# First attention of a two-layer transformer program: row maxima from 40 of 120 contraction rows, two heads in two halves of the array, causal mask added by TensorE

## Chip, core and metric

One core of a Trainium2 chip runs one launch that computes the whole program. The time is the device time of that launch in microseconds (us). Engines are named as in the profile: PE is TensorE's matmul side and PEld its weight loads, DVE is VectorE, ACT is ScalarE, POOL is GpSimd, SP is SyncE, which here only issues DMAs.

## The reference, cut to what matters

Two attention layers and two mixture-of-experts layers follow one another, each added to `x`. The change touches the first attention alone, with B = 4 sequences of T = 1024 rows of 128 values, 16 heads, each with 8 content and 32 rotary dimensions:

```python
q = jnp.concatenate([q_content, q_rope], axis=-1)      # 40 values per head
k = jnp.concatenate([k_content, k_rope], axis=-1)
scores = jnp.einsum('bhqd,bhkd->bhqk', q, k) * scale
scores = jnp.where(causal[None, None], scores, jnp.float32(-jnp.inf))
attn = jax.nn.softmax(scores, axis=-1)
out = jnp.einsum('bhqk,bhkd->bhqd', attn, v)
```

The softmax subtracts a row maximum from each score before the exponential. Any number near the maximum serves there, since it cancels between numerator and denominator.

## The kernel before

**Units.** The first attention works on 32 units: a unit is two heads of one sequence (`NU = 8 * B`). A score is a product of two fp32 numbers, each split into a high and a low part in TensorE's fp32r format. The tiles `Qp` and `Kp` (four buffers each, 128 partitions x 2 heads x 1024 columns) hold these parts stacked along the contraction: partitions 64 to 103 hold the 40 high parts of a head, 0 to 63 and 104 to 119 the cross terms high x low and low x high, and partition 120 the row maximum (against ones on the other side). SP ships them there from the rotary and content tiles with 16 DMAs per unit (L484).

**Items.** An order written out in Python (`Attn0.order`) lists the items of all engines. Per unit there are 12 `mx` items, 12 `st` items, one `mxT`, and 6 `pv`. Nearly all use a ring of three PSUM tiles `S0` to `S2` (128 x 1024, two banks, one per head): an item may be written only when the item three places earlier in the ring has been read. `mx` and `st` alternate in it, so an `mx` waits for ACT's reading of an `st` and an `st` waits for DVE's reading of an `mx`.

- `mx` (L548): queries x keys for both heads, one matmul per head with contraction over 120 partitions, to find row maxima of a unit two ahead of the one attended. Of a unit's 12 `mx` items, 4 are full (512 columns per head, no mask) and 8 are diagonal: their last 128 columns hold the causal triangle, and they have 128, 256, 384 or 512 columns, twice each.
- DVE reads a full item with one reduction over both heads (L760, to `first`). For a diagonal item it runs one fused instruction per head (L765) that adds the mask tile `later` (128 x 512, zeros and then the triangle), takes the maximum and writes the sum back to PSUM; each is followed by a short read of the accumulator into `mx`.
- `mxT` (L553, L776, L828): the maxima are transposed, negated, and sent by a DMA on POOL's queue into partition 120 of `Qp`.
- `st` (L559): keys x queries with contraction over 121 partitions, so the maximum is already taken off; ACT exponentiates it into `P` (L653), POOL zeroes the triangle (L836).
- `pv` (L577): P x V after every second `st`; four matmuls with 9 output columns each, placed in four column strips of the array.
- `ao`, `oT`: the sums are copied, transposed (L583) and divided (L785 to L791). For the next half sequence, `rope` (L540, L741 to L747, L824), `v`, `cq`, `ck` and the layer norm run beside it, and routing of earlier sequences (L233 to L307).

The lowest line that the change moves at the start is L672, a memset of `later` on DVE; `mqk`, the triangle, is loaded by SP at L462.

Of the kernel before, what the change touches and what calls it, by code (L numbers as in the profile page):

```python
# [313 lines left out]
NU = 8 * B  # L314
EARLY = 3
# [13 lines left out]
class Attn0:  # L329
    names = ("wkd", "wvd", "wo0")  # L330

    def __init__(self, p, st, route):
# [11 lines left out]
        self.later = sb("later", [128, 512])  # L344
# [112 lines left out]
def attn0_sync(p, k, sp, ye):  # L457
# [3 lines left out]
    for t, n in ((k.cos[:], "cos"), (k.sin[:], "sin"), (k.R["ck"][:], "wkr"), (k.later[:, 384:512], "mqk")):  # L461
        ye.dma_start(t, a[n]).then_inc(p.sem("d_c").h, 16)  # L462
# [4 lines left out]
    for u in range(NU):  # L467
        b, group = u // 8, u // 4
        if u >= 4:
            sp.wait_ge(p.made("st"), 12 * (u - 3))  # L470
        for name, tiles, high in (("cq", k.Q, 0), ("ck", k.K, 1)):
            dst = tiles[u % 4]
            if group:
                sp.wait_ge(p.sem("g_rope_l"), 4 * group - (2 if name == "cq" else 0))
            else:
                sp.wait_ge(p.sem("v_rope_l"), 2 if name == "cq" else 4)
            sp.wait_ge(p.done(name), b + 1)
            for h in range(2):
                r, q = 16 * (2 * u % 8 + h), 8 * (2 * u % 16 + h)
                rope, content = k.RH[name][r:r + 16].bitcast(F32), k.CH[name][q:q + 8].bitcast(F32)  # L480
                for at, many, src in ((64, 2, rope[:, high]), (96, 1, content[:, high:high + 1]), (104, 2, content),
                                      (0, 4, rope.rearrange("p a b t -> p (a b) t"))):
                    rows = dst[at:at + many * src.shape[0], h, :].bitcast(F32)
                    ye.dma_start(rows, src).then_inc(p.sem(f"d_q{u % 4}").h, 16)  # L484
# [5 lines left out]
def attn0_tensor(p, k, pe, te):  # L490
    S, A, W = p.S, p.A, k.W
    for w in k.items:
# [49 lines left out]
        elif w.kind == "mx":  # L542
# [4 lines left out]
            for h in range(2):  # L547
                ins = te.matmul(S[s][:, 512 * h:512 * h + n], Q[0:120, h, 128 * qt:128 * qt + 128],  # L548
                                K[0:120, h, 512 * part:512 * part + n], start=True, stop=True)
# [120 lines left out]
def attn0_vector(p, k, dve, ve):  # L670
    S, x = p.S, p.x
    ve.memset(k.later[:, 0:384], 0.0)  # L672
# [5 lines left out]
    for w in k.items:  # L678
# [75 lines left out]
        elif w.kind == "mx":  # L754
# [8 lines left out]
            for h in range(2):  # L763
                of = S[s][:, 512 * h:512 * h + n]
                ins = ve.tensor_tensor_reduce(out=of, in0=of, in1=k.later[:, 512 - n:512], scale=1.0, scalar=-3e38, op0=ALU.add, op1=ALU.max,  # L765
                                              accum_out=k.mx[:, h, qt:qt + 1])
# [1441 lines left out]
```

## Time and profile before

| | us |
|---|---|
| three runs | 1746.73, 1750.57, 1753.07 (median 1750.57) |
| the profiled execution | 1747.28 |
| its span, first to last instruction | 1745.5 |
| first attention in steady state | about 81 to 918 of the span |
| PE busy over the span | 1377.1 (79%) |
| DVE busy over the span | 1127.0 (65%) |
| granted TensorE clock, mean | 0.868 of 2.4 GHz |

Busy time is what the records of an engine cover. A matmul's record includes its way through the array, so a busy PE can still be waiting for nothing but latency. The clock has two levels, 1.2 and 2.4 GHz; a granted clock of 0.95 over a stretch means that it was at the lower one for a tenth of it. The chain follows the work that ended last back from the end; its shares tell which engine's work set the time.

### The profile page before, as it was taken

Reading aid. Unit: us, or ns where it says so; the run is one execution under the profiler, and the core shown is the slowest. Engines: PE = TensorE matmul, PEld = TensorE weight load, DVE = VectorE, ACT = ScalarE, POOL = GpSimd, SP = SyncE. Lnnn points to the kernel's source line nnn. Section 1 sums busy time; section 2 is a strip of 40 time slices with the busy share of each in tenths; the row PEclk is TensorE's granted clock in tenths of the full one; section 3 lists DMA queues with packets and bytes.
Section 4 is the critical chain, followed back from the end, with each engine's and each line's share of the span. In section 5 each row is a group of like instructions: output and inputs, shape, how many; then the busy total and the mean of one; then the engine's idle time right before and its main releaser. Section 6 shows DMA issues by size and latency. Waiting matters only on the chain.

```text
span 1745.5 us, 36985 instructions
## 1 busy us (share of the span) xinstructions
PE 1377.1 (79%) x13404; PEld 896.9 (51%) x13404; DVE 1127.0 (65%) x3630; ACT 703.9 (40%) x1139; POOL 688.7 (39%) x1004
## 2 busy tenths in 40 slices
PE   3487888878888888787886799959899984877881
PEld 2243434444344444443544566637677773665671
DVE  4477686776767767777673554438888775444556
ACT  1044444534444444444453033425544441113673
POOL 3022232232332332323222123357976763564664
PEclk9699999989999989999898699968988885556996
DMA  4645616356164461553702401111221112112334
GB/s 103 94 79 83 100 24 106 57 87 99 24 102 64 73 111 20 86 88 54 125 11 99 142 28 33 40 44 52 56 60 34 33 34 97 33 38 73 89 89 160
DMA packets 74151, 123.23 MB, mean 71 GB/s; under 512 B 17680, under 2 KB 46359, under 8 KB 73076
## 3 DMA queue, kind: packets, MB, share of 16 engines
q1 hardware_dynamic: 65252, 106.81, 32.2%
q0 software_dynamic: 7616, 13.59, 2.3%
q8 instruction: 109, 1.79, 0.4%
q10 hardware_dynamic: 1104, 0.48, 0.1%
q14 instruction: 70, 0.57, 0.1%
HBM read 30.47 MB, written 17.60 MB: 28 GB/s over the span
## 4 chain that ended last, share of the span: by engine, by line
PE 54%; DVE 21%; issue 6%; DMA 6%; SPq 5%; ACT 4%; POOL 3%; DVEq 0%; ACTq 0%; POOLq 0%
PE S L548 5%; DVE first L760 5%; PE A L577 5%; PE S L1016 4%; SPq L484 4%; PE S L540 4%; PE S L559 4%; PE S L1336 3%; DVE S L765 3%; PE A L1347 3%; PE S L168 2%; DMA Kp<-rck 2%; DVE tB L742 2%; PE S L1353 2%; PE A L1028 2%
## 5 line engine op out<-in xcount | busy, mean ns | idle before, releaser
L653 ACT ACTIVATE P<-S 128x1024 f32<-128x1024 f32 (+3 forms) x384 | 309.7, 809 | 406.1 <-PE S L559 403.0
L836 POOL TENSOR_SCALAR_AFFINE_SELECT P<-P 128x256 f32<-128x256 f32 (+1 forms) x256 | 115.0, 450 | 502.0 <-ACT P L653 501.9
L548 PE MATMUL S<-Kp,Qp 120*128 120x512 f32 (+3 forms) x768 | 241.8, 400 | 73.3 <-DMA Kp<-rck 43.7
L559 PE MATMUL S<-Qp,Kp 121*128 121x512 f32 (+3 forms) x768 | 239.5, 396 | 66.0 <-DVE first L760 21.7
L765 DVE CUSTOM_DVE_ANT_0 S<-S,later 128x512 f32<-128x512 f32 (+3 forms) x512 | 239.6, 513 | 59.3 <-PE S L548 58.2
L548 PEld LDWEIGHTS S<-Kp,Qp 120*128 120x128 f32 x768 | 130.3, 201 | 217.6 <-issue 101.5
L760 DVE TENSOR_REDUCE first<-S 128x2 f32<-128x1024 f32 x128 | 156.6, 1223 | 111.3 <-PE S L548 110.7
L559 PEld LDWEIGHTS S<-Qp,Kp 121*128 121x128 f32 x768 | 134.5, 199 | 139.9 <-DVE first L760 39.9
L577 PE MATMUL A<-P,V 128*9 128x512 f32 (+3 forms) x1536 | 183.9, 526 | 3.7 <-POOL P L836 3.7
L1558 POOL TENSOR_TENSOR prod<-qf,kT 128x128 f32<-128x128 f32 x160 | 78.5, 524 | 29.4 <-PE A L1347 22.2
L1984 POOL DMA_INDIRECT yq<-yq,id x71 | 69.6, 980 | 51.4 <-DVE yq L1939 34.7
L1175 POOL DMA_INDIRECT ys<-yo,id x39 | 38.1, 977 | 105.6 <-DVE yo L1155 101.7
L1016 PE MATMUL S<-w,xgT 128*128 x156 | 76.5, 613 | 2.8 <-issue 1.3
L1336 PE MATMUL S<-kT,Qm 32*32 32x64 f32 x4096 | 60.0, 228 | 19.4 <-issue 12.6
L1979 POOL DMA_INDIRECT xq<-n,posu x64 | 63.1, 986 | 23.2 <-issue 17.6
L765 DVE DVE_READ_ACCUMULATOR2_ANT mx<- 128x1 f32 x512 | 71.6, 140 | 0.0
L1146 DVE SCALAR_TENSOR_TENSOR uu<-th,S 128x512 f32<-128x512 f32 x39 | 26.8, 688 | 68.0 <-ACT th L1048 68.0
L1336 PEld LDWEIGHTS S<-kT,Qm 32*32 32x32 f32 x4096 | 46.5, 106 | 33.5 <-issue 23.1
L741 DVE TENSOR_TENSOR tA<-S,cos 128x1024 f32<-128x1024 f32 x30 | 36.7, 1224 | 37.6 <-PE S L540 37.6
L1490 DVE TENSOR_TENSOR sc<-S,near 128x1024 f32<-128x1024 f32 x32 | 39.1, 1223 | 33.1 <-PE S L1336 33.1
L1781 PE MATMUL A<-er,hq 128*128 x284 | 50.5, 300 | 7.9 <-issue 7.2
L151 POOL TENSOR_SCALAR rs<-mv 128x4 f32<-128x4 f32 (+1 forms) x36 | 7.0, 195 | 114.7 <-DVE mv L145 114.5
(316 smaller groups left out, 2786.7 us busy)
## 6 DMA issues: line engine op xcount, KB each, us to landing
Qp<-rcq SPq DMA_DIRECT2D x64, 256.0 KB
Kp<-rck SPq DMA_DIRECT2D x64, 256.0 KB
Qp<-rcq SPq DMA_DIRECT2D x64, 128.0 KB
Kp<-rck SPq DMA_DIRECT2D x64, 128.0 KB
xq<-xq SPq DMA_DIRECT2D x71, 72.0 KB, 1.9
yb<-yq SPq DMA_DIRECT2D x8, 528.0 KB, 4.8
Qp<-cq SPq DMA_DIRECT2D x64, 64.0 KB
Kp<-ck SPq DMA_DIRECT2D x64, 64.0 KB
```

The costliest lines, as they stand in the source:

```text
L484: ye.dma_start(rows, src).then_inc(p.sem(f"d_q{u % 4}").h, 16)
L540: ins = te.matmul(S[s][:, 512 * e:512 * e + 512], k.R[name][:, m:m + 128], k.xnT[:, c], start=True, stop=True)
L548: ins = te.matmul(S[s][:, 512 * h:512 * h + n], Q[0:120, h, 128 * qt:128 * qt + 128], K[0:120, h, 512 * part:512 * part + n], start=True, ...
L559: ins = te.matmul(S[s][:, 512 * h + c:512 * h + 512], K[0:121, h, 128 * kb:128 * kb + 128], Q[0:121, h, 512 * qh + c:512 * qh + 512], star ...
L577: ins = te.matmul(A[oa][o:o + 9, c:512], k.V[u // 8 % 2][:, kb, 2 * (u % 8) + h, :], k.P[(e.n - 1) % NP0][:, h, c:512], start=kb < 2, stop ...
L653: se.activation(k.P[(w.n - 1) % NP0][:, :, c:512], S[s][:].rearrange("p (j k) -> p j k", j=2)[:, :, c:512], ACT.Exp, scale=SCALE0).then_in ...
L760: ve.tensor_reduce(k.first[:, :, qt - 4], S[s][:].rearrange("p (h k) -> p h k", h=2), AX.X, ALU.max).then_inc(p.done("mx").h, 1)
L765: ins = ve.tensor_tensor_reduce(out=of, in0=of, in1=k.later[:, 512 - n:512], scale=1.0, scalar=-3e38, op0=ALU.add, op1=ALU.max, accum_out= ...
L836: ge.affine_select(P[:, :, start:c + 128], P[:, :, start:c + 128], [[0, 2], [1, wide]], ALU.is_ge, 0.0, base=start - c, channel_multiplier ...
L1016: ins = te.matmul(S[s][:, c:c + 512], k.xgT[t % NH][:], k.w1[:, bass.ds(expert[t] * 1024 + c, 512)], start=True, stop=True)
L1336: ins = te.matmul(C[32 * q:32 * q + 32, 64 * h:64 * h + 64], k.Qm[c % 2][rows, j, 128 * i + 32 * q:128 * i + 32 * q + 32], k.kT[c % 2][row ...
L1558: ins = ge.tensor_tensor(prod[:, n, :], q, kT[:, at:at + 128], ALU.mult)
```

## The change

1. `mx` contracts over 40 partitions instead of 120: only the product of high parts. For the first head they lie at partitions 64 to 103 (as before), for the second at 0 to 39 (`HIGH = (64, 0)`); its rotary cross terms move to 40 to 103. The number and sizes of the DMAs stay. The two heads of an `mx` item thus lie in different halves of the array's rows.
2. A diagonal `mx` item gets two more matmuls, one per head: a bf16 identity times the bf16 triangle, 128 columns, accumulated onto the last 128 columns of each head.
3. DVE reads every diagonal item with one reduction over both heads, which writes `mx` directly. The 512 fused instructions and their 512 accumulator reads become 256 reductions.
4. At the start DVE makes the two bf16 tiles from the loaded `mqk` (now landed in `tA`) and the identity, instead of the memset of `later`. It waits for the constants' semaphore before that, ahead of the memsets of `A`.

`st`, which computes the scores that are used, is as before.

```diff
+HIGH = (64, 0)
...
-        self.later = sb("later", [128, 512])
+        self.later, self.identb = sb("later", [128, 128], BF16), sb("identb", [128, 128], BF16)
...
-                for at, many, src in ((64, 2, rope[:, high]), (96, 1, content[:, high:high + 1]), (104, 2, content),
-                                      (0, 4, rope.rearrange("p a b t -> p (a b) t"))):
+                z = HIGH[h]
+                for at, many, src in ((z, 2, rope[:, high]), (z + 32, 1, content[:, high:high + 1]), (104, 2, content),
+                                      (40 * h, 4, rope.rearrange("p a b t -> p (a b) t"))):
...
-                ins = te.matmul(S[s][:, 512 * h:512 * h + n], Q[0:120, h, 128 * qt:128 * qt + 128],
-                                K[0:120, h, 512 * part:512 * part + n], start=True, stop=True)
+                r = slice(HIGH[h], HIGH[h] + 40)
+                ins = te.matmul(S[s][:, 512 * h:512 * h + n], Q[r, h, 128 * qt:128 * qt + 128], K[r, h, 512 * part:512 * part + n],
+                                start=True, stop=part != qt // 4)
+            if part == qt // 4:
+                pe.wait_ge(p.sem("v_masks"), 1)
+                for h in range(2):
+                    ins = te.matmul(S[s][:, 512 * h + n - 128:512 * h + n], k.identb[:], k.later[:], start=False, stop=True)
...
-    ve.memset(k.later[:, 0:384], 0.0)
+    dve.wait_ge(p.sem("d_c"), CONSTS0)
+    ve.tensor_copy(k.later[:], k.tA[:, 0, 0:128])
+    dve.wait_ge(p.sem("d_id"), 16)
+    ve.tensor_copy(k.identb[:], p.ident[:]).then_inc(p.sem("v_masks").h, 1)
+    dve.wait_ge(p.sem("v_masks"), 1)
...
-            for h in range(2):
-                of = S[s][:, 512 * h:512 * h + n]
-                ins = ve.tensor_tensor_reduce(out=of, in0=of, in1=k.later[:, 512 - n:512], scale=1.0, scalar=-3e38, op0=ALU.add, op1=ALU.max,
-                                              accum_out=k.mx[:, h, qt:qt + 1])
+            ins = ve.tensor_reduce(k.mx[:, :, qt], S[s][:].rearrange("p (h k) -> p h k", h=2)[:, :, 0:n], AX.X, ALU.max)
```

PE, early in the second unit attended (L548 is `mx`, L559 `st`, L577 `pv`, L583 the transposes of `oT`, L540 `rope`), before:

```order
67 L548 MATMUL S<-Kp,Qp 128x256 x2
68 L559 MATMUL S<-Qp,Kp 128x128 x2
69 L577 MATMUL A<-P,V 9x512 x4
70 L548 MATMUL S<-Kp,Qp 128x512 x2
71 L559 MATMUL S<-Qp,Kp 128x512 x2
72 L548 MATMUL S<-Kp,Qp 128x128 x2
73 L540 MATMUL S<-xnT,rope_cq 128x512 x2
74 L559 MATMUL S<-Qp,Kp 128x512 x2
```

The same place after (L551 is `mx`, L556 its masks, L566 `st`, L584 `pv`, L542 `rope`):

```order
87 L551 MATMUL S<-Kp,Qp 128x256 x2
88 L556 MATMUL S<-later,identb 128x128 x2
89 L566 MATMUL S<-Qp,Kp 128x128 x2
90 L584 MATMUL A<-P,V 9x512 x4
91 L551 MATMUL S<-Kp,Qp 128x512 x2
92 L566 MATMUL S<-Qp,Kp 128x512 x2
93 L551 MATMUL S<-Kp,Qp 128x128 x2
94 L556 MATMUL S<-later,identb 128x128 x2
95 L542 MATMUL S<-xnT,rope_cq 128x512 x2
96 L566 MATMUL S<-Qp,Kp 128x512 x2
```

The order of items is the same; a pair of masks stands behind each diagonal pair of `mx`, and none behind the full ones. On DVE, in the same unit, before (L741 to L747 are the rotary step):

```order
154 L765 ISA S,mx<-S,later 128x256
155 L765 ISA mx 128x1
156 L765 ISA S,mx<-S,later 128x256
157 L765 ISA mx 128x1
158 L765 ISA S,mx<-S,later 128x128
159 L765 ISA mx 128x1
160 L765 ISA S,mx<-S,later 128x128
161 L765 ISA mx 128x1
162 L769 TENSOR_TENSOR mx<-mx,first 128x2x4
163 L741 TENSOR_TENSOR tA<-S,cos 128x1024
```

and after (L774 is the new reduction; its three rows here are the items of 384, 256 and 128 columns):

```order
81 L774 TENSOR_REDUCE mx<-S 128x2 x3
82 L777 TENSOR_TENSOR mx<-mx,first 128x2x4
83 L752 TENSOR_TENSOR tA<-S,cos 128x1024
```

Four instructions per diagonal item have become one, at the same place between the others.

## Rows read from the trace of the kernel before

**Rows 1.** The page, part 1: busy us (share of span) and instructions by engine.

```profile
PE 1377.1 (79%) x13404; PEld 896.9 (51%) x13404; DVE 1127.0 (65%) x3630; ACT 703.9 (40%) x1139; POOL 688.7 (39%) x1004
```

**Rows 2.** Windows (window, us, busy of PE, PEld, DVE, ACT, POOL, clock, DMA, GB/s).

```profile
81.00:918.00 837.00, 692.07 (x3723) 364.41 (x3724) 600.97 (x1942) 377.27 (x493) 232.00 (x352) 0.95 0.47 74
410.13:436.48 26.35, 22.05 (x147) 13.49 (x147) 15.63 (x54) 12.67 (x17) 5.99 (x12) 1.00 0.53 81
634.60:662.30 27.70, 23.53 (x148) 14.02 (x147) 15.55 (x54) 12.73 (x17) 5.97 (x13) 0.94 0.49 75
720.20:748.90 28.70, 24.38 (x138) 14.62 (x139) 17.34 (x74) 11.05 (x16) 7.98 (x14) 0.88 0.79 131
600.30:634.60 34.30, 27.99 (x142) 16.48 (x143) 21.32 (x98) 11.75 (x16) 9.79 (x16) 0.80 0.77 125
```

**Rows 3.** The chain of work in the stretch 81 to 918, shares by line.

```profile
by line: PE S L548 11.3%; DVE first L760 11.0%; PE A L577 10.2%; PE S L559 7.1%; PE S L540 6.5%; DVE S L765 6.2%; issue 5.7%; SPq L484 5.3%; DMA Kp<-rck 4.4%; DVE tB L742 3.9%; DVE tA L741 3.1%; DMA Qp<-mT 2.5%; POOL rck L824 2.0%; DVE tA L
```

**Rows 4.** Groups by form (line engine op tiles shapes xcount | busy us, mean ns | idle before).

```profile
L760 DVE TENSOR_REDUCE first<-S 128x2 f32<-128x1024 f32 x128 | 156.6, 1223 | 111.3 <-PE S L548 110.7
...
L765 DVE CUSTOM_DVE_ANT_0 S<-S,later 128x512 f32<-128x512 f32 x128 | 85.9, 712 | 36.8 <-PE S L548 36.7
L765 DVE DVE_READ_ACCUMULATOR2_ANT mx<- 128x1 f32 x512 | 71.6, 140 | 0.0
...
L714 DVE TENSOR_REDUCE mv<-tB 128x8 f32<-128x256 f32 x3 | 1.3, 420 | 0.1
```

**Rows 5.** Timeline of PE and PEld (start, us, engine, line) around 422.

```profile
421.19 1.05 PE L577 MATMUL A<-P,V 128*9 128x512 f32 x8 [0.88 <-POOL P L836]
422.16 0.30 PEld L548 LDWEIGHTS S<-Kp,Qp 120*128 120x128 f32 x2 [0.86 <-issue]
422.17 0.72 PE L548 MATMUL S<-Kp,Qp 120*128 120x512 f32 x2
422.50 0.42 PEld L559 LDWEIGHTS S<-Qp,Kp 121*128 121x128 f32 x2
422.73 0.62 PE L559 MATMUL S<-Qp,Kp 121*128 121x512 f32 x2
...
423.19 0.34 PE L548 MATMUL S<-Kp,Qp 120*128 120x128 f32 x2
```

**Rows 6.** Timeline of DVE, 74.9 to 80, where nothing but maxima runs.

```profile
74.95 1.22 DVE L760 TENSOR_REDUCE first<-S 128x2 f32<-128x1024 f32 x1
76.09 0.29 DVE L765 CUSTOM_DVE_ANT_0 S<-S,later 128x128 f32<-128x128 f32 x1
...
76.54 0.73 DVE L765 CUSTOM_DVE_ANT_0 S<-S,later 128x512 f32<-128x512 f32 x1
...
77.84 0.60 DVE L765 CUSTOM_DVE_ANT_0 S<-S,later 128x384 f32<-128x384 f32 x1
...
78.87 0.46 DVE L765 CUSTOM_DVE_ANT_0 S<-S,later 128x256 f32<-128x256 f32 x1
...
79.63 0.33 DVE L765 CUSTOM_DVE_ANT_0 S<-S,later 128x128 f32<-128x128 f32 x1
```

**Rows 7.** Waits in 81 to 918: total us, times, longest; last row SP's own.

```profile
DVE first L760 <- PE S L548: 97.6, 78, 5.2
PEld S L548 <- issue: 85.0, 104, 3.0
...
SPq L484 <- POOL rck L824: 95.9, 7, 14.7
```

**Rows 8.** Timeline, later layers: small array tiles, and a 1-row matmul between 128-row ones.

```profile
1169.81 1.79 PE L1336 MATMUL S<-kT,Qm 32*32 32x64 f32 x128 [1.42 <-ACT Qm L1409]
...
1490.74 0.50 PEld L1744 LDWEIGHTS S<-abr,ones 1*128 1x128 f32 x2 [0.23 <-issue]
```

**Rows 9.** The start: DVE's first work after its memsets, and the landing of `mqk`.

```profile
12.21 0.29 DVE L676 TENSOR_SCALAR wkd<-wkd,gkv 128x128 f32<-128x128 f32 x1 [9.75 <-DMA wo<-in_wo]
...
later<-in_mqk SPq DMA_DIRECT2D x1, 64.0 KB, 7.3
```

More of the change, by code:

```diff
@@ L460, in attn0_sync @@
     ye.dma_start(p.x[:, 0:8, :], x_in[:, 0:8, :]).then_inc(p.sem("d_x").h, 16)
-    for t, n in ((k.cos[:], "cos"), (k.sin[:], "sin"), (k.R["ck"][:], "wkr"), (k.later[:, 384:512], "mqk")):
+    for t, n in ((k.cos[:], "cos"), (k.sin[:], "sin"), (k.R["ck"][:], "wkr"), (k.tA[:, 0, 0:128], "mqk")):
         ye.dma_start(t, a[n]).then_inc(p.sem("d_c").h, 16)
```

## The prediction

> **What bounds the kernel now.** I read the page's busy shares first [rows 1]: PE is covered for 79% of the span and DVE for 65%, an average over four layers that only says no engine is full. The window of the first attention comes next [rows 2], since nothing else is touched: 837 us from 81 to 918, PE 692, DVE 601, so 31 units of 27 us, and a granted clock of 0.95. Then the chain inside that window [rows 3]: PE's own lines carry 35% of it before the small ones (`mx` 11.3, `pv` 10.2, `st` 7.1, `rope` 6.5), DVE's full maxima 11.0%, its diagonal maxima 6.2% and some accumulator reads, and 11.7% lies in the refilling of `Qp` and `Kp` (SP 5.3, landing 4.4, POOL's `rck` 2.0; SP waited 95.9 us for `rck` [rows 7]). So it is no stage with one bound but a loop through the ring of three PSUM tiles: `st` waits for DVE to read an `mx`, the next `mx` follows on PE, DVE waits for that one. The waits show the other side: DVE stood idle 97.6 us for a full `mx` [rows 7]. A saving on DVE counts where the chain runs through DVE, an addition on PE where it runs through PE, and PE has more of it.
>
> How much of each kind is on the path: `mx` has 372 pairs in the window, of some 0.6 us (0.34 to 0.73 by size [rows 5]), 223 us in all, of which 11.3% of 837 or 95 us is on the chain, 42%. The 248 diagonal reads take 0.9 us each on DVE (below), 223 us, of which 52 us is on the chain, about 24% with some accumulator reads.
>
> **DVE's maxima, taken out.** Where DVE does nothing else, pairs of fused instructions start 0.45, 0.76, 1.03 and 1.30 us apart for 128, 256, 384 and 512 columns, and the reduction over 1024 columns takes 1.14 from its start to the next [rows 6]. The new reduction over 2 x 128 columns is of the form of L714, whose record is 0.42 us against 1.22 for 1024 [rows 4]: 1.04 ns a column, and the same 0.08 us of overlap. So the new items cost 0.34, 0.61, 0.87 and 1.14, and save 0.11, 0.15, 0.16 and 0.16, 0.145 on average. Times 248 that is 36 us of DVE's time, of which 24% on the path: **-9 us**, between 0 and -36. The accumulator reads go with it; 0.14 us each [rows 4] looks like more than is saved, but half of their time was already overlapped.
>
> **The matmuls of `mx`, side by side.** A pair of 512 columns that finds the array free takes 0.72 us from the weight load to the end of the second record, one of 128 in a running stream 0.34, and one of 512 there 0.62 to 0.63 [rows 5]: 384 columns more in each of two matmuls cost 0.29, so a column takes 0.38 ns, about one cycle of 2.4 GHz. That tiles of the array work at once is seen in a later layer, where 128 small matmuls of 64 columns take 1.79 us, 14 ns each [rows 8]. With the heads in different halves the second matmul runs under the first: n x 0.417 + 0.02 us less, 0.23 for 512 columns and 0.16 for a diagonal item's mean of 320. Full items: 124 x 42% = 52 on the path, x 0.23 = **-12 us**. If the halves don't overlap, this is 0 (a rival).
>
> **Switching the array's shape, added.** After `pv` in its column strips, the weights of the next `mx` start 0.08 us before the last `pv` record ends (422.16 against 422.24), while from `mx` to `st`, both over the full array, they start 0.39 us before that end (422.50 against 422.89). From the end of one pair to the end of the next it is 0.65 us across a switch (422.24 to 422.89) and 0.46 without (422.89 to 423.35) [rows 5]. A switch thus costs 0.19 us. That rows count as a change of shape too is seen where a 1-row matmul stands between 128-row ones: each such border leaves the weight side idle for 0.23 us (at the lower clock) with nothing that it waits for [rows 8]. Before, the borders are those of `pv`, two per `pv`, twelve a unit; the weight loads of `mx` stood 85.0 us in 104 waits with no releaser to name [rows 7], behind `pv` in the main. Now every `mx` is in halves and `st` and the masks are not: six entries from an `st` are new (the other six come from `pv` and were borders already) and all twelve exits. Eight exits lead to a mask, four to an `st`.
> Entries: half of the 156 `mx` items on the path, 78 x 0.19, is 15 us, but where DVE or a DMA releases the `mx` the array was empty and it costs nothing; I take **+8** of 0 to 15.
>
> **The masks, added.** A transposition of 128 columns follows its neighbour by 0.11 us, weights included, which is the nearest thing (four in 0.63 us with the way through the array); the columns alone are 0.053. So two masks cost 0.11 to 0.22, and the border before them 0.15 to 0.19. Against that goes the 0.16 us of the overlap. Net +0.10 to +0.25 for a diagonal item, x 248 x 42% = 104 on the path: +10 to +26, taken as **+16**, in the middle, since no row has a bf16 weight load. The Trainium skill ("TensorE: Matmul & The Clock Gate", weight-path perf modes) says that loads of 128 bf16 weights run at about twice the speed of others; by it this would be near +10 instead. No row here shows it.
>
> **Start.** `mqk` is issued at about 3.3 us and lands 7.3 us later; DVE was idle until 12.21 for other weights [rows 9]. Two casts of some 0.3 us and two memsets of 0.5 fit before that within 0.3 us: **0**, at most +0.3. The DMAs are the same in number and bytes.
>
> **At an unchanged clock** the sum is -9 - 12 + 8 + 16 = **+3 us**, between about -40 and +30.
>
> **The clock, the largest term.** The granted clock in this stage is at its lower level for a tenth of the time. It falls where PE has little to stream, and units with the same work show the price: 26.35 us at 1.00 against 27.70 at 0.94 [rows 2]. The second was at the lower level for 2 x 0.06 x 27.7 = 3.3 us and lost 1.35, 0.4 us per us. The change takes streaming off PE without making the stage shorter: per unit, 12 pairs of 384 columns are 3.8 us of streaming, halved by the overlap to 1.9; 16 masks give back 0.85; and 18 new borders cut pauses of 0.1 to 0.2 us into what is left. That is over 1 us of streaming less in 27, with more pauses; at the lower level the pauses also make it harder to return. In this trace the better filled units hold 1.00, those with a long thin stretch at their end 0.88 and 0.80 [rows 2]. I take the middle one of these as the stage's new mean, 0.88 for 0.95. With T the new length: T = 837 + 0.4 x (2 x 0.12 x T - 84), T = 889, +52 us. The 11.7% of the chain that runs through DMAs and POOL doesn't stretch with the clock: **+45 us**. At 0.92 it would be +19, at 0.80 +105.
>
> Sum: 1747.3 (the profiled execution) + 3 + 45 = 1795; the profiled one is 3.3 us under the median, so **1799** against the median of 1750.6.
>
> **The rivals.**
> A (the forecast), 0.56: clock 0.85 to 0.91 in the stage, 1775 to 1825.
> B, heavier: each fall lasts since borders keep PE from filling at the lower level, clock 0.80, +105 and the masks at their upper bound: 1840 to 1865. For it: the unit at 0.80 took 34.3 us; against: every unit has a `rope` stretch in which PE is full. 0.06.
> C, a wash: the clock holds at 0.94 to 0.95 and the sum above stands alone: 1745 to 1756. For it: nearly all that is taken away was short, and each step still has `st` and `pv`. The Trainium skill's page on TensorE's clock gate, in the table "Why this matters for your kernels", asks for no more than that there be no long idle gap between bursts; the pauses added here are short, so by that rule the clock would stay and this case come out. The trace doesn't bear it out well: the clock fell in units where PE was covered for four fifths of the time. 0.15.
> D, faster: DVE decides. The wait of `st` for DVE is the last one in more places than the chain shows, and the 36 us saved there count whole, with the overlap's 12, against masks at +10 that hide in DVE's shorter reads; the clock holds. 1705 to 1740, say 1722. It decides from the point where DVE's reads, not PE, end last in over two thirds of the steps; DVE is covered 72% of the window, PE 83%, which speaks against. 0.15.
> E, the halves take turns: it doesn't do what it says. Then the array's stream doesn't thin and the clock holds, but the -12 is gone and the diagonal items lose 0.16 more, 104 x 0.16 = 17: +3 + 12 + 17 = +32, 1783. 0.08.
>
> **How the numbers follow.** A, B and E are slower by over 0.3% (about 5 us, what a measurement of this kernel can tell from no change), 0.70; C is the same, 0.15; D is faster, 0.15. The range leaves out D and most of B: 1742 to 1850, with the bounds of the mask and of the clock inside it. A's own range is 1775 to 1825.
>
> **What would show it.** The diagonal reductions at 0.42 to 1.22 us with DVE's busy time in the stage down by 80 to 100 us show the first step. `mx` pairs starting within some ns of each other show the halves; a start 0.2 us apart shows E. Weight loads of `st` and of the masks that start under 0.1 us before the end of the `mx` records show the borders. The stage's granted clock decides between A, B and C: 0.88 makes A, 0.95 with about 840 us makes C. The forecast is wrong if the clock stays and the stage is shorter, or if the stage is longer at the same clock by more than 30 us.

## The result, and the profile after

| | before | after |
|---|---|---|
| median of four runs, us | 1748.65 | 1786.44 |
| lowest and highest | 1743.32, 1753.07 | 1779.35, 1791.18 |
| profiled execution | 1747.28 | 1785.56 |
| first attention, from the first to the last load of maxima into `Qp` | 837.3 | 883.8 |

The changed kernel is slower, ratio 1.021 with a 95% interval of 1.017 to 1.026. One slow execution of `same_half` and one of `border_full` are left out of their medians and ratios below. The forecast was 1799, in a range of 1742 to 1850.

The page's part 1 of the kernel after, which answers to [rows 1]:

```profile
PE 1469.4 (82%) x13916; PEld 898.5 (50%) x13916; DVE 1094.3 (61%) x2863; ACT 703.9 (39%) x1139; POOL 692.2 (39%) x1004
```

DVE did less, PE is covered longer. The windows of the kernel after, with the columns of [rows 2]: the stage, its last three units, one unit in its middle, and the layers behind it.

```profile
82.20:966.00 883.80, 788.21 (x4227) 368.59 (x4227) 568.03 (x1198) 377.94 (x494) 231.89 (x352) 0.85 0.45 70
906.10:966.00 59.90, 56.90 (x369) 24.87 (x368) 41.77 (x91) 31.90 (x43) 13.23 (x29) 1.00 0.22 34
427.90:459.90 32.00, 31.40 (x163) 16.06 (x161) 14.62 (x30) 12.94 (x17) 6.03 (x14) 0.68 0.49 72
966.00:1783.80 817.80, 644.23 (x9575) 510.06 (x9574) 486.84 (x1596) 314.67 (x633) 446.74 (x633) 0.80 0.22 66
```

The stage, the same last three units, and the layers behind, of the kernel before:

```profile
81.60:918.90 837.30, 692.97 (x3731) 365.31 (x3731) 600.97 (x1942) 377.43 (x494) 232.03 (x353) 0.95 0.47 73
856.20:918.90 62.70, 53.19 (x321) 27.89 (x319) 45.56 (x163) 32.31 (x43) 13.24 (x30) 1.00 0.25 40
918.90:1745.50 826.60, 650.25 (x9575) 512.25 (x9573) 485.11 (x1596) 315.14 (x633) 443.11 (x633) 0.79 0.21 65
```

Three things stand here. The stage is 46.5 us longer and its granted clock fell from 0.95 to 0.85: PE was at its lower level for 30% of it instead of 10%. Where the clock held at 1.00, the changed kernel is the *faster* one, 59.9 against 62.7 us for three units. And a unit of 163 matmuls took 32.0 us at a clock of 0.68, where one of the same mix without the 16 masks took 26.35 at 1.00 before [rows 2]. The loss is in the clock, and in these last units it hides a gain.

The clock falls in both kernels at one kind of place: at the start of every fourth unit PE waits for `Kp` to land, mostly some 3 to 5 us. The timelines of PE show it, of the kernel before and of the kernel after:

```profile
723.34 1.22 PE L548 MATMUL S<-Kp,Qp 120*128 120x512 f32 x2 [3.77 <-DMA Kp<-rck]
```

```profile
761.18 0.74 PE L551 MATMUL S<-Kp,Qp 40*128 40x512 f32 x2 [4.36 <-DMA Kp<-rck]
```

The kernel before, windows of 716 to 740, around this wait:

```profile
716.00:723.00 7.00, 2.73 (x17) 1.14 (x16) 3.12 (x15) 1.84 (x2) 1.37 (x3) 1.00 0.78 119
723.00:730.00 7.00, 6.63 (x22) 3.94 (x23) 2.63 (x5) 1.47 (x3) 0.80 (x2) 0.51 0.76 111
730.00:740.00 10.00, 9.57 (x67) 6.57 (x66) 8.56 (x39) 3.66 (x7) 1.84 (x4) 1.00 0.77 126
```

The kernel after, windows of 754 to 788, around the same wait:

```profile
754.00:761.00 7.00, 2.68 (x18) 0.89 (x17) 2.57 (x9) 1.73 (x2) 1.41 (x3) 1.00 0.72 111
761.00:768.00 7.00, 6.82 (x28) 3.49 (x28) 3.00 (x3) 1.47 (x3) 0.80 (x2) 0.52 0.78 116
768.00:778.00 10.00, 10.00 (x44) 5.17 (x44) 5.98 (x26) 3.53 (x6) 1.85 (x4) 0.50 0.78 124
778.00:788.00 10.00, 10.00 (x44) 6.40 (x41) 3.39 (x10) 2.62 (x3) 3.30 (x4) 0.50 0.82 133
```

Before, the clock is back at 2.4 GHz 7 us behind the wait. After, PE is covered almost without a gap and yet stays at 1.2 GHz for 27 us. Covered is not the same as streaming.

The kernel after also has falls with no such wait ahead of them. The windows of the kernel after, 420 to 450, in the unit at 0.68:

```profile
420.00:430.00 10.00, 9.06 (x61) 4.72 (x61) 7.73 (x22) 4.80 (x6) 3.39 (x6) 1.00 0.76 125
430.00:440.00 10.00, 10.00 (x44) 5.07 (x43) 3.88 (x6) 3.38 (x6) 2.14 (x5) 0.51 0.59 85
440.00:450.00 10.00, 10.00 (x45) 4.37 (x44) 3.95 (x11) 3.72 (x6) 2.10 (x4) 0.50 0.76 119
```

The timeline of PE and PEld of the kernel after, one diagonal item of 512 columns with its masks and the `st` behind it, which answers to [rows 5]:

```profile
418.12 0.19 PEld L551 LDWEIGHTS S<-Kp,Qp 40*128 40x128 f32 x2 [0.42 <-ACT P L660]
418.13 0.50 PE L551 MATMUL S<-Kp,Qp 40*128 40x512 f32 x2
418.56 0.11 PEld L556 LDWEIGHTS S<-later,identb 128*128 128x128 bf16 x2 [0.24 <-issue]
418.56 0.28 PE L556 MATMUL S<-later,identb 128*128 128x128 bf16 x2
418.63 0.30 PEld L566 LDWEIGHTS S<-Qp,Kp 121*128 121x128 f32 x2
418.65 0.71 PE L566 MATMUL S<-Qp,Kp 121*128 121x512 f32 x2
```

The pair of `mx` takes 0.50 us, so the halves do work at once. The weights of the masks start 0.07 us before the `mx` records end, those of `st`, with no border ahead, 0.21 us before the masks' records end: the border holds them. From the start of the pair to the end of the masks it is 0.71 us, where the pair alone took 0.72 before.

DVE's groups by form, kernel after, and its waits in 82 to 966, with PEld's wait at the new border ([rows 4, 7]):

```profile
L774 DVE TENSOR_REDUCE mx<-S 128x2 f32<-128x1024 f32 x64 | 78.1, 1221 | 46.4 <-PE S L556 44.3 <-issue 2.1
L774 DVE TENSOR_REDUCE mx<-S 128x2 f32<-128x256 f32 x64 | 27.1, 424 | 15.6 <-PE S L556 15.5
```

```profile
PEld S L551 <- issue: 143.3, 210, 3.3
DVE first L771 <- PE S L551: 112.8, 85, 6.3
DVE mx L774 <- PE S L556: 99.2, 111, 4.1
```

DVE waits longer for PE than before, 212 us for full and diagonal items together against 156. So does the chain in the stage tell it; kernel after, shares by line, against [rows 3]:

```profile
by line: PE S L566 14.4%; PE A L584 12.5%; PE S L551 11.6%; PE S L542 6.6%; DVE first L771 6.0%; SPq L486 5.0%; DMA Kp<-rck 4.3%; issue 4.1%; PE S L556 4.0%; DVE tB L753 3.7%; DVE tA L752 2.9%; DMA Qp<-mT 2.9%; DVE mx L774 2.2%; POOL rck L8
```

PE's five lines carry 49% (35% before, without masks), the two maxima of DVE 8.2% (17.2%).

### The profile page after: what moved, and what is told of

It reads as the page before. It is cut to its first block, busy times and chain, and to the rows that moved or that the text cites. A ratio compares the mean times of both kernels' runs of the same rounds, so it can differ in the third digit from the quotient of the medians.

```text
span 1783.8 us, 37241 instructions
## 1 busy us (share of the span) xinstructions
PE 1469.4 (82%) x13916; PEld 898.5 (50%) x13916; DVE 1094.3 (61%) x2863; ACT 703.9 (39%) x1139; POOL 692.2 (39%) x1004
## 4 chain that ended last, share of the span: by engine, by line
PE 62%; DVE 15%; DMA 6%; issue 5%; SPq 5%; ACT 4%; POOL 2%; DVEq 1%; POOLq 0%; ACTq 0%
PE S L566 7%; PE A L584 6%; PE S L551 6%; PE S L1024 4%; PE S L542 4%; SPq L486 4%; PE S L1344 3%; DVE first L771 3%; PE S L168 2%; PE A L1355 2%; DMA Kp<-rck 2%; PE S L556 2%; DVE tB L753 2%; PE A L1789 2%; PE S L1361 2%
## 5 line engine op out<-in xcount | busy, mean ns | idle before, releaser
L566 PE MATMUL S<-Qp,Kp 121*128 121x512 f32 (+3 forms) x768 | 280.9, 453 | 45.8 <-DVE tB L753 20.6
L774 DVE TENSOR_REDUCE mx<-S 128x2 f32<-128x1024 f32 (+3 forms) x256 | 209.9, 822 | 102.2 <-PE S L556 99.2
L551 PE MATMUL S<-Kp,Qp 40*128 40x512 f32 (+3 forms) x768 | 193.1, 501 | 62.7 <-DMA Kp<-rck 47.2
L551 PEld LDWEIGHTS S<-Kp,Qp 40*128 40x128 f32 x768 | 80.8, 208 | 258.8 <-issue 160.8
L584 PE MATMUL A<-P,V 128*9 128x512 f32 (+3 forms) x1536 | 199.8, 566 | 0.4 <-POOL P L844 0.4
L566 PEld LDWEIGHTS S<-Qp,Kp 121*128 121x128 f32 x768 | 139.0, 221 | 115.6 <-issue 47.7
L556 PE MATMUL S<-later,identb 128*128 128x128 bf16 x512 | 79.3, 242 | 0.0
L556 PEld LDWEIGHTS S<-later,identb 128*128 128x128 bf16 x512 | 30.1, 100 | 47.4 <-issue 35.7
```

Source lines behind the costliest of these rows:

```text
L551: ins = te.matmul(S[s][:, 512 * h:512 * h + n], Q[r, h, 128 * qt:128 * qt + 128], K[r, h, 512 * part:512 * part + n], start=True, stop=par ...
L556: ins = te.matmul(S[s][:, 512 * h + n - 128:512 * h + n], k.identb[:], k.later[:], start=False, stop=True)
L566: ins = te.matmul(S[s][:, 512 * h + c:512 * h + 512], K[0:121, h, 128 * kb:128 * kb + 128], Q[0:121, h, 512 * qh + c:512 * qh + 512], star ...
L584: ins = te.matmul(A[oa][o:o + 9, c:512], k.V[u // 8 % 2][:, kb, 2 * (u % 8) + h, :], k.P[(e.n - 1) % NP0][:, h, c:512], start=kb < 2, stop ...
L774: ins = ve.tensor_reduce(k.mx[:, :, qt], S[s][:].rearrange("p (h k) -> p h k", h=2)[:, :, 0:n], AX.X, ALU.max)
```

## Experiments

The theory: the loss is the clock, because `mx` keeps less of the array at work, while at an unchanged clock the change costs little. Kernels that ran together share runs of the kernel before; the layers behind the stage took between 818 and 845 us in the profiled executions though nothing in them differs, so below the stage itself is read, and the ratio, rather than the absolute time. The groups ran on three chips, on which the kernel before took 1748.78 us (`masks_full` to `twice`), 1767.50 (`rows60` to `border_full`) and 1745.26 (the four with `fill`); it was not profiled beside them, so a small difference of stage or clock between two groups proves little by itself. All windows have the columns of [rows 2] and, where two are shown, are the stage and its last three units.

### The parts apart: the masks alone, the 40 rows alone

`masks_full` keeps the masks on PE and the single reduction, but `mx` contracts over 120 rows again, with the layout of the kernel before (the diff shows the rows alone):

```diff
-                r = slice(HIGH[h], HIGH[h] + 40)
+                r = slice(0, 120)
```

> The changed kernel with mx as it was before (120 rows, both heads over the full array, rows of Qp and Kp laid out as before): only the masks on TensorE and the single reduction on DVE are kept. Theory (the clock): no streaming is taken off PE, masks add 0.85 us of it per unit, and the new borders between halves and full array are gone, so the granted clock in the first attention stays at 0.94 or above, and DVE's saving shows: 1735 to 1750, that is 0 to 15 us under before. Rival (borders and masks cost it at any clock): the masks alone cost PE some 0.15 us on each of 256 items, so this is slower than before by 10 to 20 us, at 0.95 of the clock.

Measured: 1751.27 us, ratio 0.998 (0.995 to 1.002). The clock is as the theory had it; the gain in time that it named didn't show.

```profile
79.70:918.70 839.00, 722.47 (x4227) 388.30 (x4227) 564.12 (x1198) 376.01 (x494) 231.84 (x353) 0.95 0.47 74
855.70:918.70 63.00, 56.29 (x369) 29.96 (x367) 41.52 (x91) 31.98 (x43) 13.27 (x30) 1.00 0.27 41
```

`halves_only` is the other part: the kernel before, its `mx` on 40 rows in two halves with the layout of the kernel after, its masks on DVE.

```diff
+HIGH = (64, 0)
...
-                ins = te.matmul(S[s][:, 512 * h:512 * h + n], Q[0:120, h, 128 * qt:128 * qt + 128],
-                                K[0:120, h, 512 * part:512 * part + n], start=True, stop=True)
+                r = slice(HIGH[h], HIGH[h] + 40)
+                ins = te.matmul(S[s][:, 512 * h:512 * h + n], Q[r, h, 128 * qt:128 * qt + 128],
+                                K[r, h, 512 * part:512 * part + n], start=True, stop=True)
```

> The kernel before with only the matmuls of mx changed: 40 rows, the two heads in different halves of the array; masks and maxima on DVE as before. Theory (the clock): streaming is taken off PE without even the masks to give some back, so the clock in the stage is at most what the changed kernel has, 0.80 to 0.86, and the time is at least that of the changed kernel, 1780 to 1810. Rival (the masks are the cost): without masks the overlap of the heads wins and this is faster than before, 1735 to 1745.

Measured: 1805.77 us, ratio 1.028 (1.022 to 1.034), as the theory had it.

```profile
83.90:989.10 905.20, 797.47 (x3731) 360.27 (x3731) 609.60 (x1942) 378.83 (x494) 232.07 (x352) 0.80 0.44 68
929.50:989.10 59.60, 53.94 (x321) 22.63 (x320) 45.88 (x163) 31.93 (x43) 13.17 (x29) 1.00 0.22 34
```

The two parts come apart cleanly. The masks are a wash: no loss of clock, and three units of 63.0 against 62.7 us, so DVE's shorter reads pay for 496 more matmuls and no more. All of the loss, and all of the gain in the last three units (59.6 against 62.7), comes from the 40 rows in two halves. With the masks on PE the clock is 0.85, without them 0.80: they are work on the full array, and here that helps.

### Fewer columns at work, or fewer rows?

Side by side, `mx` streams for half of the time. If that is what lowers the clock, streaming as long as before should restore it. `same_half` puts both heads in one half, so that they go one after the other (the rotary cross terms of both at 0 to 63):

```diff
-HIGH = (64, 0)
+HIGH = (64, 64)
...
-                                      (40 * h, 4, rope.rearrange("p a b t -> p (a b) t"))):
+                                      (0, 4, rope.rearrange("p a b t -> p (a b) t"))):
```

> The changed kernel with the second head's high parts at partitions 64 to 103 as well, so both heads' matmuls lie in the same half of the array and take turns; borders, masks and the single reduction stay. Theory (the clock): columns stream as long as before, so the clock is back near 0.94 if a half-filled array counts like a full one, and the time is 1755 to 1775, under the changed kernel although each mx pair takes longer by up to 0.21 us. Rival (borders and masks cost it, not the clock): slower than the changed kernel by 10 to 25 us, 1795 to 1810. If a half-filled array counts for half, the clock falls further too, to 0.80 or less, and the time is over 1800: this tells which of the two it is.

Measured: 1864.01 us, ratio 1.062 (1.058 to 1.067), with the third of the outcomes named.

```profile
81.80:1057.70 975.90, 908.78 (x4227) 438.50 (x4227) 572.53 (x1198) 380.10 (x494) 232.22 (x353) 0.79 0.41 63
992.90:1057.70 64.80, 62.19 (x370) 29.15 (x369) 42.58 (x91) 32.21 (x43) 13.27 (x30) 1.00 0.21 32
```

`twice` issues each pair of `mx` twice, side by side, the second over the first:

```diff
-            for h in range(2):
+            for again in range(2):
+                for h in range(2):
...
-                                start=True, stop=part != qt // 4)
+                                    start=True, stop=again == 0 or part != qt // 4)
```

> The changed kernel with each pair of mx matmuls issued twice into the same place (the second overwrites the first), the heads side by side each time. The work of PE is larger by 0.05 to 0.21 us per item, with nothing taken away. Theory (the clock): the streaming that the overlap took off is put back with both halves filled, so the clock in the stage rises from 0.85 to 0.93 or more and the time falls below that of the changed kernel, 1755 to 1775, though PE has more to do. Rival (PE's own time is what was added): slower than the changed kernel, 1795 to 1820.

Measured: 1846.35 us, ratio 1.055 (1.048 to 1.061), slower than even its rival had it.

```profile
82.90:1030.80 947.90, 877.21 (x4971) 427.13 (x4971) 571.99 (x1198) 379.73 (x494) 231.94 (x353) 0.83 0.42 65
965.90:1030.80 64.90, 62.25 (x441) 29.21 (x439) 42.59 (x91) 32.17 (x43) 13.24 (x30) 1.00 0.20 32
```

My theory as I had put it falls here. Both kernels stream as many columns one after another as `masks_full`, and both have a lower clock than it (0.79 and 0.83 against 0.95), not a higher one. The timelines of both in their last units, at full clock, show that they do what they say: `same_half` at 1002, then `twice` at 1000.

```profile
1002.67 0.73 PE L551 MATMUL S<-Kp,Qp 40*128 40x512 f32 x2
```

```profile
1000.52 0.73 PE L552 MATMUL S<-Kp,Qp 40*128 40x512 f32 x4
```

A pair in one half takes 0.73 us, four matmuls in two halves take 0.73 too, against 0.50 for the pair side by side. So what matters for the clock must be how much of the array's height works, or the pauses at the borders. Three kernels vary the rows alone: instead of 40 rows a head, 56 (64 to 119) and 64 (0 to 63). The operands are other rows of the same tiles, so the maxima are those of a different partial sum; columns, instructions and borders stay.

```diff
-                r = slice(HIGH[h], HIGH[h] + 40)
+                r = slice(64, 120) if h == 0 else slice(0, 64)
```

`rows60` is this edit in the kernel after, `twice60` in `twice`, `halves60_dve` in `halves_only`.

> The changed kernel with more rows in each mx matmul and nothing else: partitions 64 to 119 for the first head (its high parts and content cross terms) and 0 to 63 for the second (its high parts and 24 rows of rotary cross terms, part of them only, harmless in a maximum that cancels). Columns, borders, masks, DVE's work are those of the changed kernel, and so is the length of a unit at a clock of 1.00, some 20.0 us for the last ones. Theory R (what holds the clock is also how many rows of the array work): with 120 rows busy per pair instead of 80 the clock of the stage rises from 0.85 to 0.90 or more, and the time falls to 1730 to 1765. Theory P (only the time that columns stream and the pauses at the borders count): clock 0.85 and 1780 to 1795 as for the changed kernel.

> The kernel with mx pairs issued twice, now with 56 and 64 rows instead of 40. Theory R: the clock, 0.83 with 40 rows, rises to 0.92 or more, and the time from 1846 to 1760 to 1785 (PE still has the pairs twice, some 0.7 to 1.6 us more per unit than the changed kernel at a clock of 1.00). Theory P: it stays at 0.83 and 1835 to 1860.

> The kernel before with mx in halves, 56 and 64 rows, masks and maxima on DVE as before. Theory R: clock from 0.80 (40 rows) to 0.87 or more, time from 1806 to 1745 to 1780. Theory P: clock 0.80, 1790 to 1815. Against rows60 it shows what the masks on TensorE are worth when the rows are the same.

Measured, beside a kernel before of 1767.5 us on that chip: `rows60` 1788.71, ratio 1.014 (1.010 to 1.018); `twice60` 1797.53, 1.018 (1.014 to 1.021); `halves60_dve` 1805.97, 1.021 (1.017 to 1.025). The stages of `rows60`, `twice60` and `halves60_dve` in this order:

```profile
80.00:941.80 861.80, 762.23 (x4226) 354.79 (x4227) 567.54 (x1198) 377.61 (x494) 231.85 (x352) 0.88 0.46 72
```

```profile
80.90:952.80 871.90, 781.67 (x4971) 379.26 (x4971) 570.14 (x1198) 378.23 (x494) 231.84 (x352) 0.94 0.46 71
```

```profile
81.70:957.40 875.70, 751.39 (x3731) 337.21 (x3731) 608.47 (x1942) 378.00 (x494) 232.04 (x353) 0.86 0.45 70
```

Same instructions, more rows: the clock goes from 0.85 to 0.88, from 0.83 to 0.94, from 0.80 to 0.86, and the stage is 22, 76 and 29.5 us shorter, each against a run on another chip. Of the ratios only that of `twice60` is clear of its counterpart's (1.018 against 1.055); those of the other two have intervals that overlap. What settles it for `rows60` is the pair `fill_rows60` and `fill_after` below, which ran side by side. The matmuls are not quicker for it: the last three units of `twice60` take 64.8 us against 64.9. In time none of the three came into the range of theory R; in clock only `twice60` did, and `rows60` (0.90 expected) and `halves60_dve` (0.87) stayed just under it, so rows are not all. `rows60` and `twice60`, side by side on one chip, differ only in the second issue of the pairs, and the clock goes from 0.88 to 0.94: columns count too, once the rows are there. By the rows that work at once while `mx` streams, the kernels line up: 120 in `masks_full` (0.95) and `twice60` (0.94), 120 for half as long in `rows60` (0.88), 80 for half as long in the kernel after (0.85), 80 in `twice` (0.83), 40 in `same_half` (0.79). That is an order seen in six kernels and not a rule. What these kernels can't separate is the number of rows from the values in them, since the other rows hold low parts too.

`border_full` asks for the pauses alone: `masks_full` with a matmul of 8 columns on 40 rows ahead of each pair of `mx`, overwritten by it, which makes two borders more at each of the six items of a unit that follow an `st`, and one more at each of the six that follow a `pv`, where a border was already: 18 a unit, as many as the kernel after has. (The expectation counts 24 against 18.)

```diff
+            te.matmul(S[s][:, 0:8], Q[0:40, 0, 128 * qt:128 * qt + 128], K[0:40, 0, 0:8], start=True, stop=True)
```

> The kernel with masks on TensorE and mx over 120 rows of the full array (1751, clock 0.95), with one more matmul ahead of every mx pair: 40 rows in the lower half, 8 columns, into the place that the pair overwrites. It adds two borders per item, 24 a unit against 18 in the changed kernel, and next to no streaming, and takes nothing away. Theory P: the pauses at the borders hold the clock down, 0.88 or less, and the time is over 1800. Theory R: the clock stays at 0.93 or above and only the pauses themselves show, 12 x 0.2 to 0.4 us per unit where PE is on the path: 1775 to 1805.

Measured: 1833.51 us, ratio 1.040 (1.037 to 1.043).

```profile
86.70:992.30 905.60, 838.14 (x4598) 469.57 (x4597) 576.81 (x1198) 379.20 (x494) 231.89 (x352) 0.92 0.43 67
923.60:992.30 68.70, 65.03 (x405) 36.33 (x404) 43.08 (x91) 32.22 (x43) 13.22 (x29) 1.00 0.20 30
```

The clock, 0.92, lies between the two theories; the time is over 1800, as theory P had it, but for another reason. If the borders cost clock, it is little (0.95 without, on another chip): `same_half` has the same 18 new borders, the same masks and the same columns one after another, and runs at 0.79. In time the small matmuls are dearer: three units take 68.7 against 63.0 us, 5.7 for 36 of them and 54 borders, **0.11 us a border at most**, with all that the small matmul and its weights take. `same_half` prices the border without them: its last three units differ from those of `masks_full` in rows and borders alone, 64.8 against 63.0, 1.8 for 54 borders, **0.03 us a border**.

### Keeping the clock up at the wait for `Kp`

If the clock falls because PE idles for `Kp`, work in that wait should hold it. Ahead of the first `mx` of every fourth unit, at 7 places, 16 matmuls of 120 rows and 512 columns on the unit before's `Qp` and `Kp` are issued into the PSUM tile that this `mx` overwrites; their results are never read.

```diff
+            if u and u % 4 == 0 and qt == 7 and part == 0:
+                Qo, Ko = k.Q[(u - 1) % 4], k.K[(u - 1) % 4]
+                for j in range(16):
+                    te.matmul(S[s][:, 512 * (j % 2):512 * (j % 2) + 512], Qo[0:120, j % 2, 0:128], Ko[0:120, j % 2, 0:512], start=True, stop=True)
```

Four kernels have it: `fill_before`, `fill_after`, `fill_rows60` and `fill_masks_full`, each the kernel of that name with this edit.

> The kernel before with 16 more matmuls (120 rows, 512 columns, 3.4 us at 2.4 GHz) ahead of the first mx of every fourth unit, seven times in all, written to the PSUM tile that the mx then overwrites. PE stands there for 2.8 to 4.2 us, waiting for the landing of Kp, and the clock falls within a few us of it. Theory (these waits are what starts the falls): the clock in the stage rises from 0.95 to 0.97 or above, and more PE work makes the kernel faster, by 5 to 20 us. Rival (the falls have other causes, or the filling only delays mx): clock 0.95 and 0 to 10 us slower.

> The changed kernel with the same 16 matmuls at the same seven places. Theory: the falls at these waits go and with them the long stretches at the lower level behind them, the clock rises from 0.85 to 0.92 or more and the time falls from 1786 by 25 to 50 us, to or below the kernel before. Rival: the stream with 40 rows falls and stays low by itself; the clock stays under 0.88 and less than 15 us is gained.

> rows60 (mx in halves with 56 and 64 rows) with the same 16 matmuls at the same places. Theory: with the falls gone and the rows there, the clock is 0.95 or more, and the side-by-side matmuls and the shorter reads show alone: 10 to 30 us faster than the kernel before. Rival: as before or slower.

> masks_full (mx over 120 rows of the full array, masks on TensorE, one reduction) with the same 16 matmuls. It had the clock of the kernel before and its time. Theory: it gains what fill_before gains, 5 to 20 us, and ends level with it; fill_rows60 is faster than it by the side-by-side matmuls, 15 to 30 us. Rival: no gain.

| | us (before beside it 1745.26) | ratio, 95% | stage, us | clock |
|---|---|---|---|---|
| `fill_before` | 1734.35 | 0.991 (0.989 to 0.994) | 818.2 | 0.99 |
| `fill_masks_full` | 1731.93 | 0.993 (0.990 to 0.997) | 822.3 | 0.99 |
| `fill_rows60` | 1754.93 | 1.005 (1.002 to 1.008) | 857.1 | 0.91 |
| `fill_after` | 1785.34 | 1.021 (1.015 to 1.026) | 875.2 | 0.88 |

The timeline of PE and the windows of `fill_before` at the same wait as above:

```profile
710.01 3.89 PE L549 MATMUL S<-Kp,Qp 120*128 120x512 f32 x16
714.00 0.73 PE L552 MATMUL S<-Kp,Qp 120*128 120x512 f32 x2
```

```profile
708.00:714.00 6.00, 5.40 (x28) 3.27 (x28) 2.08 (x10) 1.26 (x2) 1.37 (x3) 1.00 0.68 122
714.00:721.00 7.00, 6.36 (x42) 4.15 (x44) 4.95 (x20) 2.49 (x5) 0.80 (x2) 1.00 0.75 109
```

`fill_before` and `fill_masks_full` gained as the theory had it, and `fill_after` went as its rival. `fill_rows60` was to be 10 to 30 us faster than the kernel before and 15 to 30 faster than `fill_masks_full`; it was slower than both, by 0.5% and by 23 us. Idle PE at that wait is shown as the cause of about four fifths of the time that the kernel before spends at the lower level: with the wait filled, the stage runs at 0.99 instead of 0.95 and is 19.1 us shorter. Between `fill_after` and `fill_rows60` only the rows differ, and both ran on one chip: the clock goes from 0.88 to 0.91, the stage is 18.1 us shorter and the ratios are clear of each other, so more rows in `mx`, or what they hold, do raise the clock. `fill_before` and `fill_masks_full` beat both kernels. In the changed kernel the same filling gives back 8.6 us of stage and nothing measurable in the time: it loses its clock elsewhere as well, in stretches where PE is covered. Behind the stage's first wait for `Kp` (5.59 us at 87, which isn't filled) no idle time of PE in the stage is longer than 1.8 us, and the clock falls all the same. The windows of `fill_after`, 764 to 782, show one such fall:

```profile
764.00:770.00 6.00, 5.90 (x44) 3.03 (x42) 4.99 (x18) 2.84 (x6) 1.66 (x4) 1.00 0.72 117
770.00:776.00 6.00, 5.82 (x43) 3.67 (x41) 4.79 (x17) 1.37 (x4) 0.98 (x3) 0.95 0.76 112
776.00:782.00 6.00, 6.00 (x29) 3.12 (x27) 2.62 (x10) 3.34 (x4) 3.99 (x4) 0.50 0.86 150
```

The masks on PE give nothing on top of the filling that could be measured.

## Why the prediction came out right

**The clock as the largest term: right, and too small.** It said 0.88 and +45 us; it was 0.85. What a microsecond at the lower level costs is seen in two kernels with the same instructions, after and `rows60`: 22.0 us of stage for 2 x 0.15 x 883.8 = 265 us at that level against 2 x 0.12 x 861.8 = 207, which is 0.38 (a rough value, since the clock is rounded to hundredths and the two ran on different chips). The unit at 0.68 gives 0.32: 2 x 0.32 x 32.0 = 20.5 us at the lower level, and 6.5 more than 26.35 less the 0.9 that a unit gained. The prediction had 0.4, cut by DMAs to 0.35, and that holds. With 0.35 the 181 us more at the lower level are about +63.

**The sum at an unchanged clock: too high by 10 to 20 us.** 46.5 less 63 leaves -17, where +3 stood, as rough as the price is. Read directly it is less: the last three units at 1.00 say -0.9 us a unit, and seven others that hold 1.00 in both kernels, each compared at its own place in the order, between -0.46 and +0.55, -0.15 in the mean; over 31 units this makes -7, and then the clock cost some 53. So the sum was 7 to 17 us below zero and the clock's term 53 to 63 instead of 45. The two errors hid each other: the stage grew by 46.5 for a forecast of 48. That the clock would fall and be the largest term was foreseen; that the stage came out within 2 us is luck. The total was forecast 13 us too high because the unchanged layers happened to be 8.8 us shorter in the profiled execution after, and the median lies 0.9 above that execution, not 3.3.

Within that sum, term by term:

- *DVE's maxima, -9.* The reductions take 1221 to 424 ns as read off [rows 4]. Busy time in the stage fell by 33 us (601.0 to 568.0); the working had 36, and only the later sentence "80 to 100" was wrong, which forgot the overlap that the working had counted. `masks_full` shows that gain and mask cost cancel.
- *Side by side, -12 for full items.* 0.50 for 0.72 us, as worked out. In sum with the borders, `halves_only` gained 1.0 us a unit in its last three, at full clock.
- *Borders, 0.19 us each where on the path.* This is the price that failed. It was read from one pair of intervals around one `pv` [rows 5]. That there is a border was right: the next weights start 0.07 us before the last record ends, where they started 0.39 us before without one. But its price was 0.03 us by `same_half`, and 0.11 at most by `border_full` with everything that comes with it. The +8 becomes +1 to +5, and the masks' term, which holds the borders behind `mx`, shrinks too.
- *Masks, +0.10 to +0.25 an item, border included.* From the start of the pair to the end of the masks it is 0.71, 0.65, 0.60 and 0.55 us for 512 to 128 columns, against 0.72, 0.62, 0.51 and 0.34 to 0.40 for the pair alone before: +0.07 to +0.08 in the mean. The +16 becomes +7 to +8, and with the borders the sum is an estimated -8 to -13. Part of it is that bf16 weights load faster; groups by form of PEld, kernel after:

```profile
L551 PEld LDWEIGHTS S<-Kp,Qp 40*128 40x128 f32 x768 | 80.8, 208 | 258.8 <-issue 160.8 <-DMA Kp<-rck 22.7 <-ACT P L660 18.4
L556 PEld LDWEIGHTS S<-later,identb 128*128 128x128 bf16 x512 | 30.1, 100 | 47.4 <-issue 35.7
```

100 ns against 208. The Trainium skill's page "TensorE: Matmul & The Clock Gate" (weight-path perf modes) states that factor of two; the trace agrees, and its near +10 for this term was the better value.

- *Start, 0.* DVE's first work on loaded weights starts at 12.40 us, 0.19 later than [rows 9], and nothing is left of it afterwards.

**The reason given for the clock: half right.** "The change takes streaming off PE" named columns. With the columns given back (`same_half`, `twice`) the clock did not return; with more rows it rose, to 0.88, and with rows and columns both to 0.94 (`twice60`). The prediction gave rows no part in it. Its other cause, the borders, is small (0.95 to 0.92 at most). What it said of the return to the higher level is where much of the time went (7 us at the lower one behind a wait became 27), but the thin array prevents it more than the pauses do: with the same number of new borders, `same_half` runs at 0.79 and `border_full` at 0.92. Nor does it take a long thin stretch for a fall, as the prediction had read from [rows 2]: the unit at 0.68 fell with PE covered for 9.06 of the 10 us before. The fillings of [rows 2] don't bear that reading out either, PE being covered for 84%, 85%, 85% and 82% of its units at 1.00, 0.94, 0.88 and 0.80. That 0.88 lay near the 0.85 measured is luck to that extent.

**The rivals.** E is out: the pairs overlap. D is out, DVE's wait for PE grew. C, a clock that holds and an unchanged time, came out where the 40 rows were left away, in `masks_full`. The rule behind it, the Trainium skill's page "TensorE: Matmul & The Clock Gate", table "Why this matters for your kernels", asks for bursts without long idle gaps. It agrees with `fill_before`, whose filled wait kept the clock. It doesn't foretell the kernel after, which was at the lower level with PE covered for 10.00 of 10.00 us; here the measurement decides. What isn't shown is how much of that covered time the array streamed. B's clock of 0.80 came out in `halves_only`, without B's time, since the price of the fixed work was lower than it had.

## What to carry to other kernels

When work is taken off TensorE, ask what it leaves the array doing: a pair of matmuls with a third of the rows and two thirds of the time made the last units 0.9 us quicker at full clock, and the stage of 837 us 47 us longer through the clock. Look at where the granted clock falls and what the engine did there before trimming anything; here 112 matmuls whose results nobody reads, put into seven waits, gained 0.9%. Two opposite errors can make a sum come true, so compare the stage at full clock, and its clock, each on its own, and kernels that ran on the same chip.

## What the runs showed of the hardware

- The granted clock depends on how many rows of the array work, or on what is in them, not on streamed columns alone: the same 4971 matmuls ran at 0.83 with 40 rows and at 0.94 with 56 and 64 in their `mx`; on one chip, `fill_after` and `fill_rows60` ran at 0.88 and 0.91. Columns count beside it: 0.88 in `rows60`, 0.94 in `twice60`.
- The granted clock fell with no long wait ahead: 1.00 in 420 to 430 of the kernel after, PE covered for 9.06 us, then 0.51 with it covered for 10.00.
- Matmuls in the lower and the upper 64 rows overlap: a pair of 512 columns takes 0.50 us in two halves and 0.73 in one.
- Changing the array's shape holds the next weights until 0.07 us before the last record's end (0.39 without) and costs 0.03 us on average in the last three units of `same_half`, at most 0.11 in those of `border_full`.
- Whether rows or values lower the clock stays open; a kernel with zeros in added rows would tell it and was not run.
